# Lower triangle of batched Gram matrices on one core: turned tiles handed to TensorE in halves, laps of two tiles, no late loads

## What is computed

```python
r_inputs: (2048, 64, 256) float32
Z = jnp.einsum('bnd,bmd->bnm', inputs, inputs)      # a 64 x 64 Gram matrix per batch
li, lj = jnp.tril_indices(64, k=-1)
return Z[:, li, lj]                                 # (2048, 2016): the strict lower triangle, packed by rows
```

## Time and profile before

| | |
|---|---|
| median of 3 runs | 401.72 us (401.25 to 402.3) |
| profiled execution, its own time | 403.43 us |
| its span | 401.6 us |
| busy: TensorE matmul, VectorE, ScalarE, GpSimd | 365.2, 362.3, 178.4, 197.7 us |
| DMA | 151.01 MB, mean 376 GB/s |

### The profile page before, as it was taken

The page is one execution under the profiler, slowest core; times in us unless marked ns, Lnnn a source line. Parts: engine busy times, 40 slices in busy tenths (PEclk is TensorE's granted clock), DMA queues, the critical chain, the costliest instruction groups (busy, mean ns, idle before and its releaser), DMA issues.

```text
span 401.6 us, 68674 instructions
## 1 busy us (share of the span) xinstructions
PE 365.2 (91%) x33024; PEld 359.8 (90%) x33024; DVE 362.3 (90%) x240; ACT 178.4 (44%) x821; POOL 197.7 (49%) x974
## 2 busy tenths in 40 slices
PE   4439999999999999999999999998999899998960
PEld 4439999999999999999999999998989899998960
DVE  3417899999999999999999998989999798998995
ACT  0011224555445544465445654453554344455463
POOL 1000047282833866086817475283835738184585
PEclk9999999999999999999999999999999999999995
DMA  8299999999999999999999999999999999998417
GB/s 319 105 351 427 420 422 423 420 405 421 422 425 402 422 425 421 422 415 425 420 424 413 421 417 419 352 399 417 381 425 360 425 370 422 403 366 339 138 31 206
DMA packets 21274, 151.01 MB, mean 376 GB/s; under 512 B 2688, under 2 KB 2816, under 8 KB 4864
## 3 DMA queue, kind: packets, MB, share of 16 engines
q1 hardware_dynamic: 18752, 135.77, 83.8%
q10 hardware_dynamic: 2496, 14.97, 9.6%
HBM read 134.22 MB, written 16.52 MB: 375 GB/s over the span
## 4 chain that ended last, share of the span: by engine, by line
DVE 43%; DMA 34%; issue 13%; PE 8%; DVEq 0%
DVE x_turned L233 38%; DMA x_in<-x_dram 34%; PE bank_set L311 8%; DVE row_halves L250 3%; DVE x_in L257 1%; DVE packed_rows L153 1%; DVE packed_rows L142 0%; DVE x_turned L262 0%; DVEq L249 0%; DVEq L232 0%; DVEq L74 0%; DVEq L282 0%
## 5 line engine op out<-in xcount | busy, mean ns | idle before, releaser
L311 PE MATMUL bank_set<-x_turned 32*64 32x64 f32 x33024 | 365.2, 237 | 23.3 <-issue 15.1
L311 PEld LDWEIGHTS bank_set<-x_turned 32*64 32x64 f32 x33024 | 359.8, 132 | 28.5 <-issue 16.1
L233 DVE STREAM_TRANSPOSE x_turned<-x_in 128x2048 f32<-128x2048 f32 x128 | 287.9, 2280 | 33.8 <-PE bank_set L311 18.4
L153 POOL COPY packed_rows<-row_halves 32x32 f32<-32x32 f32 (+30 forms) x930 | 190.0, 204 | 198.3 <-DVE row_halves L250 98.6
L342 ACT COPY products<-bank_set 128x512 f32<-128x512 f32 (+1 forms) x91 | 68.4, 758 | 153.1 <-PE bank_set L311 141.0
L250 DVE STREAM_TRANSPOSE row_halves<-products 128x1024 f32<-128x1024 f32 x60 | 72.2, 1205 | 0.0
L142 ACT COPY packed_rows<-row_halves 128x32 f32<-128x32 f32 (+30 forms) x465 | 61.4, 220 | 16.6 <-DVE row_halves L250 16.5
L148 ACT COPY packed_rows<-row_halves 128x128 f32<-128x128 f32 x240 | 54.0, 299 | 27.8 <-DMA y_dram<-packed_rows 16.1
L342 ACT ACT_TABLE_LOAD x1 | 1.3, 1283 | 19.6 <-PE bank_set L311 19.6
L153 POOL COPY packed_rows<-x_in 32x32 f32<-32x32 f32 (+30 forms) x31 | 4.9, 209 | 0.1
L257 DVE STREAM_TRANSPOSE x_in<-products 128x512 f32<-128x512 f32 (+1 forms) x5 | 4.8, 998 | 0.0
## 6 DMA issues: line engine op xcount, KB each, us to landing
x_in<-x_dram SPq DMA_DIRECT2D x128, 1024.0 KB, 16.2
y_dram<-packed_rows ACTq DMA_DIRECT2D x22, 504.0 KB, 9.2
y_dram<-packed_rows ACTq DMA_DIRECT2D x6, 252.0 KB
y_dram<-packed_rows ACTq DMA_DIRECT2D x24, 63.0 KB
y_dram<-packed_rows SPq DMA_DIRECT2D x2, 504.0 KB, 4.7
y_dram<-packed_rows SPq DMA_DIRECT2D x1, 380.0 KB
y_dram<-packed_rows ACTq DMA_DIRECT2D x1, 380.0 KB
y_dram<-packed_rows SPq DMA_DIRECT2D x1, 124.0 KB
```

Source lines behind the costliest of these rows:

```text
L153: return copy(packed_rows[first:first + BLOCK, group % 2, :, at + BLOCK:at + i], halves(group)[first + BLOCK:first + HALF, i, :, 0:i - BLOCK])
L233: nc.vector.transpose(x_turned[:, j].rearrange("p c b s (h u n v) -> p u v (c b s h) n", h=ROWS // BLOCK, u=PAIRS, v=PAIR), x_in[:, k]).th ...
L311: done = nc.tensor.matmul(bank_sets[s][side * HALF:(side + 1) * HALF, g, at, :].rearrange("r (n u v) -> r u n v", u=PAIRS, v=PAIR), rows, ...
```

## The change

TensorE's loop gets laps of 2 tiles, each with a PSUM set of its own; the tile of zeros goes. `x_turned` holds 2 tiles in place of 3. A tile is turned by two instructions of 1024 elements, chunks 0 to 3 and chunks 4 to 7, each with its own semaphores, and TensorE multiplies the first half of the chunks for both slots before the second half, so that two sums are open in a bank at a time. ScalarE copies each tile by itself (512 elements). No load waits for TensorE or ScalarE any more. `PACK_LAG` goes from 19 to 20.

```diff
-    LATE = 4
-    LAP = 3
-    LAPS = -(-TILES // LAP)
-    BLANK = LAPS * LAP - TILES
-    SET_TILES = (2, 1)
-    SETS = len(SET_TILES)
+    LAP = 2
+    LAPS = TILES // LAP
+    SETS = LAP
+    PARTIALS = 2
+    PARTIAL = CHUNKS // PARTIALS
...
-    PACK_LAG = 2 * PIECE_LAG - 3
+    PACK_LAG = 2 * PIECE_LAG - 2
...
                 if t >= IN_RING:
                     lap, j = place(t - IN_RING)
-                    sync.wait_ge(turned[j], (lap + 1) * LAP)
-                elif t == LATE:
-                    lap, j = place(0)
-                    sync.wait_ge(tile_multiplied[j], lap + 1)
-                elif t == LATE + 1:
-                    lap, j = place(0)
-                    sync.wait_ge(kept[set_of(j)[0]], (lap + 2) * LAP)
+                    sync.wait_ge(turned[j][PARTIALS - 1], (lap + 1) * LAP)
...
-                if lap > 0:
-                    dve.wait_ge(tile_multiplied[j], lap)
-                nc.vector.transpose(
-                    x_turned[:, j].rearrange("p c b s (h u n v) -> p u v (c b s h) n", h=ROWS // BLOCK, u=PAIRS, v=PAIR),
-                    x_in[:, k]).then_inc(turned[j], LAP)
+                for h in range(PARTIALS):
+                    chunks = slice(h * PARTIAL, (h + 1) * PARTIAL)
+                    if lap > 0:
+                        dve.wait_ge(multiplied[j][h], lap)
+                    nc.vector.transpose(
+                        x_turned[:, j, chunks].rearrange(
+                            "p c b s (h u n v) -> p u v (c b s h) n", h=ROWS // BLOCK, u=PAIRS, v=PAIR),
+                        x_in[:, k].rearrange("p (r d) -> p r d", r=JOINED)[
+                            :, :, chunks.start * BLOCK:chunks.stop * BLOCK]).then_inc(turned[j][h], LAP)
...
-                pe.wait_ge(turned[j], count)
-                s, in_set = set_of(j)
-                for slot in range(SLOTS):
-                    at = in_set * SLOTS + slot
...
+                for h in range(PARTIALS):
+                    pe.wait_ge(turned[j][h], count)
+                    for slot in range(SLOTS):
+                        last_slot = h == PARTIALS - 1 and slot == SLOTS - 1
...
+                        for c in range(h * PARTIAL, (h + 1) * PARTIAL):
+                            if last_slot and c == CHUNKS - 2:
+
+                                pe.wait_ge(kept[1 - j], count)
...
+                                        start=c == 0 and slot == 0, stop=c == CHUNKS - 1 and slot == SLOTS - 1)
+
+                    done.then_inc(multiplied[j][h], 1)
...
-                act.wait_ge(tile_multiplied[j + SET_TILES[s] - 1], lap + 1)
+                lap, s = place(t)
+                group, in_group = divmod(t, GROUP_TILES)
+                act.wait_ge(multiplied[s][PARTIALS - 1], lap + 1)
```

More of the change, by code:

```diff
@@ L97, in gram_lower_triangle @@
         loaded = [semaphore(f"loaded{k}") for k in range(IN_RING)]
-        turned = [semaphore(f"turned{j}") for j in range(LAP)]
+        turned = [[semaphore(f"turned{j}_{h}") for h in range(PARTIALS)] for j in range(LAP)]
         kept = [semaphore(f"set_kept{s}") for s in range(SETS)]
-        tile_multiplied = [semaphore(f"tile_multiplied{j}") for j in range(LAP)]
+        multiplied = [[semaphore(f"multiplied{j}_{h}") for h in range(PARTIALS)] for j in range(LAP)]
         rows_turned = semaphore("rows_turned")
@@ L113, in place, with wait_kept @@
         def place(t):
-            return divmod(t + BLANK, LAP)
-        def set_of(j):
-            return (0, j) if j < SET_TILES[0] else (1, j - SET_TILES[0])
+            return divmod(t, LAP)
+        def wait_kept(engine, t):
+            lap, s = place(t)
+            engine.wait_ge(kept[s], (lap + 2) * LAP)
         def piece_rows(piece):
@@ L204, in _ @@
                 pool.sem_inc(kept[s], LAP)
-            for j in range(BLANK):
-                nc.gpsimd.memset(x_turned[:, j, CHUNKS // 2:CHUNKS], 0.0).then_inc(turned[j], LAP - 1)
             for group in range(GROUPS):
@@ L240, in turn_rows @@
                 if piece == 0:
-                    lap, j = place((group + 1) * GROUP_TILES - 1)
-                    s = set_of(j)[0]
-                    dve.wait_ge(kept[s], (lap + 2) * LAP)
+                    wait_kept(dve, (group + 1) * GROUP_TILES - 1)
                 if group > 0:
@@ L259, in turn_last_rows @@
                     products[:, (GROUPS - 1) % KEPT_RING, rows, run * BLOCK:(run + 1) * BLOCK])
-            for j in range(BLANK):
-                nc.vector.memset(x_turned[:, j, 0:CHUNKS // 2], 0.0).then_inc(turned[j], 1)
             turned_rows = 0
@@ L272, in _ @@
             for run in range(RUNS):
-                lap, j = place((GROUPS - 1) * GROUP_TILES + (run + 1) * GROUP_TILES // RUNS - 1)
-                s = set_of(j)[0]
-                dve.wait_ge(kept[s], (lap + 2) * LAP)
+                wait_kept(dve, (GROUPS - 1) * GROUP_TILES + (run + 1) * GROUP_TILES // RUNS - 1)
                 if run < RUNS - 1:
@@ L318, in multiply @@
-                done.then_inc(tile_multiplied[j], 1)
+                for h in range(PARTIALS):
+                    pe.wait_ge(turned[j][h], count)
+                    for slot in range(SLOTS):
+                        last_slot = h == PARTIALS - 1 and slot == SLOTS - 1
+                        if j == LAP - 1 and last_slot:
+                            pe.reg_add(count, count, LAP)
+                        for c in range(h * PARTIAL, (h + 1) * PARTIAL):
+                            if last_slot and c == CHUNKS - 2:
+                                pe.wait_ge(kept[1 - j], count)
+                            for g in range(QUADRANTS):
+                                for side in range(SIDES):
+                                    rows = x_turned[g * BLOCK:(g + 1) * BLOCK, j, c, slot, side]
+                                    done = nc.tensor.matmul(
+                                        bank_sets[j][side * HALF:(side + 1) * HALF, g, slot, :].rearrange(
+                                            "r (n u v) -> r u n v", u=PAIRS, v=PAIR),
+                                        rows,
+                                        rows.rearrange("d (h u e) -> d u h e", h=ROWS // BLOCK, u=PAIRS),
+                                        start=c == 0 and slot == 0, stop=c == CHUNKS - 1 and slot == SLOTS - 1)
+                    done.then_inc(multiplied[j][h], 1)
@@ L329, in _, with keep @@
         def _(act):
-            def keep(lap, s):
-                j = SET_TILES[0] * s
-                act.wait_ge(tile_multiplied[j + SET_TILES[s] - 1], lap + 1)
[L334 to L348, removed]
+            def keep(t):
+                lap, s = place(t)
+                group, in_group = divmod(t, GROUP_TILES)
+                act.wait_ge(multiplied[s][PARTIALS - 1], lap + 1)
+                if group >= KEPT_RING and in_group == 0:
+                    act.wait_ge(rows_turned, (group - KEPT_RING + 1) * PIECES)
+                nc.scalar.copy(
+                    products[:, group % KEPT_RING, :, in_group * PER_SIDE:(in_group + 1) * PER_SIDE].rearrange(
+                        "p i (g b) -> p i g b", b=SLOTS),
+                    bank_sets[s][:, :, 0:SLOTS, :].rearrange("p g b i -> p i g b")).then_inc(kept[s], LAP)
             def pack(n):
@@ L374, in _ @@
             few = 0
[L375 to L388, removed]
+            for t in range(TILES):
+                keep(t)
+                if n >= (stores + 1) * PIECES * 4:
+                    store_whole(stores)
+                    stores += 1
+                    few = len(FEW_LANES) if by_few(stores - 1) else 0
+                elif few > 0:
+                    store(act, stores - 1, slice(0, PACKED), FEW_LANES[-few:][:1])
+                    few -= 1
+                while n + PACK_LAG < 2 * (t + 1):
+                    pack(n)
+                    n += 1
             for n in range(n, LAST_HOME):
```

## The result

The changed kernel takes **404.61 us** (median of 6 runs, 404.01 to 406.0), the kernel before 402.04 us in the same runs (401.25 to 403.02): ratio 1.0071, 95% interval 1.0047 to 1.0094. It is slower by 0.7%, where I had forecast 0.5% faster (399.8 against 401.72).

A forecast was written before the change was run, and what follows sets the result against it. The load queue was taken to set the end, with TensorE's code fetches setting the early part. The profiled 403.43 less 1.9 us gave 401.5; the runs' median, 1.7 lower, gave 399.8 us, range 396.3 to 405.5.

The forecast's parts named there:

- the count of stores: Load queue after load 30 lands at 88.5: 97 loads and 13 stores at 3.8 us, ending at 378.9.
- ScalarE's waits: ScalarE's waits for old stores, up to 4.62 us, expected to vanish; effect nothing, with 2 us as bound.
- signs that I had named for being wrong: TensorE continuous only after 31, VectorE's pattern over 5.75 us, or TensorE waiting for ScalarE.
- the lead: VectorE's gain at tile 11, turned at 50.2 instead of 51.21: 1.0 us; last load then 1.8 to 2.0 us earlier.
- X: Time when TensorE, past its code fetches, runs continuously: 27.3 against 29.82 before, bounds 25.2 to 30.6.
- the one-for-one rule: The change is worth how much earlier VectorE gets going, one for one.
- Rivals 2 and 3: TensorE's code fetches: behind all eight loads, 408 us, chance 0.1; or first one before TensorE starts, 395.5 us, 0.07.
- Early loads: Without the hold the load queue is 7 us ahead but can't stay there; idle time moves to 30 to 85 us.
- The halves: VectorE's turns of 1024 elements: 1.13 us each, pattern 5.65 us, 0.07 more a tile; nothing lost under the queue's pace.
- rival 1: VectorE becomes the bound if a half costs over 1.14 us; at 1.16, 405.9 us; chance 0.13.
- From X to the stores: TensorE's pace of 2.785 us a tile: tile 11 turned at X + 22.9 = 50.2, first store at 85.8.
- Rivals 1 and 4: VectorE becomes the bound, 405.9 us, chance 0.13; or the hold only moved idle time, 403.1 us, 0.2 with ScalarE losses.

The follow-up runs named there:

- e1: Changed kernel with the store of group 13 issued two ScalarE copies later (behind tile 124 instead of 122): 402.62 us, ratio to the kernel before 1.0013.
- e2: Kernel before, with one quarter pack of ScalarE moved one copy earlier, so the store of group 13 is issued earlier: 404.73 us, ratio 1.0062.
- e5: Changed kernel with the old hold on loads 4 and 5 back and the store of group 13 two copies later: 399.37 us, ratio 0.9938.
- e3: Changed kernel with the old hold back: load 4 waits until tile 0 is multiplied, load 5 until it is copied: 401.01 us, ratio 0.9973.
- e4: Kernel before without its hold on the early loads: 407.75 us, ratio 1.015.
- e6: Kernel before, with each tile turned by two instructions of 1024 elements, both announced by the second: 402.84 us, ratio 1.0016.
- e7: As e5, but tiles turned and multiplied whole, with the ring of two turned tiles kept: 403.19 us, ratio 1.0016.

## Why the prediction was wrong

**That the kernel is slower, and not level with the one before, comes from one term, the count of stores.** "97 loads at 2.485 and 13 stores at 3.8" behind a load 30 that lands at 88.5 makes 13 stores in all up to the last load, the number of the kernel before. After the change there are 14: with a copy per tile ScalarE issues the store of group 13 behind tile 122, at 372.4, and not behind tiles 122 and 123, at 377.5. The one that the sum lacks is at its head. It puts the first store at 85.8, with load 30 landing at 88.5 as if no store had been issued before; the first store was issued at 81.48 before and at 77.36 after:

```profile
81.48 0.85 ACTq L160 DMA_DIRECT2D y_dram<-packed_rows  x2
...
77.36 0.86 ACTq L157 DMA_DIRECT2D y_dram<-packed_rows  x2
```

So load 30 landed behind a store, at 93.3 (94.1 before). The rest of the sum held: from there to load 127, at 383.4, are 290.0 us, 97 loads at 2.485 and 13 stores at 3.8; before it was 286.7 us, with 12 stores. I had seen that quarter stores go out faster and used it only for ScalarE's waits; I did not ask what a store that comes earlier collides with. The term is some 4 us in the queue and an estimated 2.3 at the end, since VectorE was 1.8 us behind its last load before. e1 and e2 show it from both sides: 2.0 us back in the one, 2.6 us lost in the other. None of the signs that I had named for being wrong appeared: TensorE was continuous well before 31, the pattern was under 5.75, and TensorE didn't wait for ScalarE.

**That it isn't faster comes from a second term, the lead.** With 13 stores e1 took 402.62 us, level with before and still 2.8 above the forecast. The forecast turned a start 2.5 us earlier into an end 1.9 us earlier. In the traces load 30 landed only 0.8 us earlier than before, and VectorE's lead at tile 11, forecast as 1.0 us, was 0.5 and had turned into a lag of 0.6 by tile 24. VectorE at tile 24, before and after:

```profile
87.70 2.27 DVE L233 STREAM_TRANSPOSE x_turned<-x_in 128x2048 f32<-128x2048 f32 x1
...
88.28 4.58 DVE L224 STREAM_TRANSPOSE x_turned<-x_in 128x1024 f32<-128x1024 f32 x4
```

At the end VectorE came to tile 127 2.4 us behind its load in e1 and e5, and not 1.8. I had read the chain of the earlier trace rows as if the last load released the last two turns; they began at 380.36, before it landed, and that slack was not in the sum.

**The start** was right: X at 27.51 against 27.3, and the one-for-one rule from there to the time held for a change of the start alone, in e3 (3.3 us earlier, 3.6 faster) and e4 (4.9 later, 5.6 slower). It didn't hold across the whole change, which also altered what follows X. Rivals 2 and 3 are out: no fetch waited for all eight loads, and none came early. The Trainium skill (Runtime: NRT & Kernel Launch, section Instruction fetch mechanics) calls the crossing of a block mostly hidden; every crossing of a first lap was seen here, 1.2 to 1.5 us idle at an empty queue and 3.4 to 5.1 with loads queued.

**Early loads** were worth nothing by themselves, as argued. **The halves'** price and the 5.65 pattern were right, and e6 shows that by themselves they don't reach the end (rival 1 is out). What I left out is that they are needed: e7. **ScalarE's** waits for old stores vanished as forecast (16.1 us before, none after).

**From X to the stores** I was 0.5 us short at tile 11 (50.7 against 50.2) and 0.9 more at tile 24. TensorE's lap is 5.60 us, not 5.57, and tile 12 comes 3.6 us behind tile 11, not 3.4. From X to the turn of tile 24 it took 57.9 us before, 58.7 in e6 (the halves alone) and 60.8 after: some 0.8 us are the halves, the other 2 us the ring and the laps of two. The waits for loads on VectorE came back at 288 us, not at 340.

**Rivals 1 and 4** named times to either side of the measured one (405.9 and 403.1), by ways that weren't taken: a half cost 1.13 us, and X was not 30.6.

**What stays open.** With 13 stores in both, e1 is level with the kernel before, though TensorE is continuous over 2 us earlier; the traces place the loss between X and tile 24, and how it divides between the ring and the laps was not tried. Why a few shares of the late loads lag by 10 us no run shows, nor whether placing the stores otherwise would remove that. Single executions of one kernel also differ by 2 to 4 us in what their stores cost the queue (e1: 401.58 to 405.97), for which I have no cause.

## What to carry to other kernels

When loads set the end, count what the DMA engines carry up to the last item that is waited for, in the new order too: a store that is issued 5 us earlier for good reasons can go out beside the last load, though that was issued first, and delay it by nearly its whole length. See also whether the engines are full at that point; here a quarter of their time was left to a few late shares. Here TensorE's first pass through its loop waited for code, longer with loads queued on the DMA engines; holding back loads that would only have filled the ring cost nothing and brought the loop to speed earlier. A hold, a store's place and the halves are separate edits, and tried one by one they showed a version (e5) that is faster than both.

## What the hardware showed

- TensorE's code came in blocks of 128 pairs of weight load and matmul. A new block began 3.5 to 3.7 us after the one before with an empty load queue and 5.6 to 7.4 with four to eight 1 MB loads queued, far less than such a queue takes to empty (some 20 us).
- A transpose of 1024 elements per partition followed by another held VectorE for 1.13 us, one of 2048 for 2.19 (2.24 in e7). A single row of 1024 lasts 1.20 us, longer than the distance to the next.
- A load of 1 MB took 2.485 us in the queue, and a group's store, also 1 MB, some 3.8, by the landings of loads 30 and 127 (94.1 and 380.7 with 12 stores between, 93.3 and 383.4 with 13): half as much again.
- The 16 steps in which a load lands drifted apart: within 1 to 2 us on average over the first eight loads, 11 to 15 us over the last eight. In their tail, with nothing else issued, the loads moved 105 GB/s (before, 370 to 377.5) and 133 (after, 369 to 372.4).
